# Segment sums of a graph layer: runs of ten edges added up on VectorE, four products of sums per group on TensorE in place of 20

## What is computed

```python
h = relu(layernorm(x))
m_in = concat([h[src], h[dst], edge_attr])            # 160 per edge
msg  = silu(m_in @ W1 + b1) @ W2 + b2                 # 64 per edge
a    = softmax(silu(m_in @ Wa1 + ba1) @ Wa2 + ba2)    # one weight per edge, over ALL edges
agg  = segment_sum(msg * a, dst)                      # per node
out  = x + silu(concat([h, agg]) @ Wu1 + bu1) @ Wu2 + bu2
```

## Time and profile before

| | |
|---|---|
| runs, median of 3 | 2097.85 us (2091.92 to 2098.32) |
| the profiled execution, whole | 2096.55 us |
| its span | 2094.9 us |
| busy share of the span | PE 45%, DVE 52%, ACT 45%, POOL 73% |
| granted TensorE clock, mean | 0.688 of full |
| DMA | 228.43 MB, mean 109 GB/s |

### The profile page before, as it was taken

One profiled execution on the slowest core, in us unless ns is written; L12 is line 12 of the kernel. 1 busy time (PEld: TensorE's weight loads), 2 busy tenths in 40 slices (PEclk: granted clock), 3 DMA queues, 4 the chain that ended last, 5 costly groups with the idle time before them and its releaser, 6 DMA issues.

```text
span 2094.9 us, 21031 instructions
## 1 busy us (share of the span) xinstructions
PE 939.0 (45%) x6771; PEld 878.7 (42%) x6771; DVE 1098.9 (52%) x2367; ACT 933.7 (45%) x1107; POOL 1530.1 (73%) x1628
## 2 busy tenths in 40 slices
PE   6444444444434444444444444444434444444446
PEld 4344444433334444444434444444334344444334
DVE  5555555554554555555455545555545554554556
ACT  3544444454444444444444444444444444444443
POOL 2777777777777777777777777777777777777772
PEclk9667666666666676666666666667666666667668
DMA  7644444444444444444444444444443444444422
GB/s 199 155 122 107 105 110 107 105 105 105 105 111 114 109 105 111 107 105 105 105 105 107 115 112 105 107 109 105 105 105 105 105 116 112 107 105 112 105 69 51
DMA packets 101990, 228.43 MB, mean 109 GB/s; under 512 B 45184, under 2 KB 65460, under 8 KB 91636
## 3 DMA queue, kind: packets, MB, share of 16 engines
q1 hardware_dynamic: 47588, 120.63, 22.2%
q0 software_dynamic: 51584, 105.75, 19.9%
q10 hardware_dynamic: 2704, 0.66, 0.1%
HBM read 218.91 MB, written 8.00 MB: 108 GB/s over the span
## 4 chain that ended last, share of the span: by engine, by line
POOL 72%; issue 24%; PE 2%; DVE 1%; DMA 1%; ACTq 0%; ACT 0%; POOLq 0%; DVEq 0%
POOL p_rows L404 72%; PE bank L584 1%; DMA p_rows<-p_tab,src_all 0%; PE bank L577 0%; PE bank L728 0%; PE bank L738 0%; ACTq L438 0%; DMA q_tab<-s 0%; DMA out<-s 0%; DVE stat L773 0%; DVE bank L917 0%; DVE prod L900 0%; PE bank L677 0%; DVE lgb L926 0%; DVE lg L902 0%
## 5 line engine op out<-in xcount | busy, mean ns | idle before, releaser
L404 POOL DMA_INDIRECT p_rows<-p_tab,src_all x1612 | 1523.1, 945 | 529.3 <-issue 490.1
L636 PE MATMUL bank<-hot,v 128*65 128x96 f32 x3200 | 450.8, 329 | 850.9 <-DVE v L907 850.9
L636 PEld LDWEIGHTS bank<-hot,v 128*65 128x65 f32 x3200 | 435.9, 203 | 870.7 <-DVE v L907 870.7
L917 DVE TENSOR_TENSOR bank<-bank,p_rows 128x512 f32<-128x512 f32 (+1 forms) x403 | 269.4, 669 | 871.5 <-DMA p_rows<-p_tab,src_all 863.7
L524 ACT ACTIVATE s<-bank 128x512 f32<-128x512 f32 x403 | 240.4, 597 | 1021.1 <-DVE bank L917 1020.2
L622 PE MATMUL bank<-q_win,comb 128*128 128x128 f32 x3224 | 442.6, 295 | 266.1 <-ACT s L524 259.5
L622 PEld LDWEIGHTS bank<-q_win,comb 128*128 128x128 f32 x3224 | 407.9, 206 | 287.4 <-ACT s L524 264.7
L492 ACT ACTIVATE comb<-dst_b,row_of 96x1024 f32<-96x1024 int32 (+1 forms) x162 | 217.4, 1342 | 24.8 <-DMA dst_b<-dst_row 24.8
L498 ACT ACTIVATE comb<-comb,ones 96x1024 f32<-96x1024 f32 (+1 forms) x162 | 218.7, 1350 | 2.7
L870 DVE TENSOR_TENSOR hot<-bank,rel 128x960 f32<-128x960 f32 x162 | 178.2, 1139 | 0.0
L900 DVE TENSOR_TENSOR prod<-s,bank 128x512 f32<-128x512 f32 (+1 forms) x162 | 131.6, 813 | 18.6 <-ACT s L524 16.1
(11 more groups left out here) (110 smaller groups left out, 299.1 us busy)
## 6 DMA issues: line engine op xcount, KB each, us to landing
dst_b<-dst_row SPq DMA_DIRECT2D x80, 960.0 KB
p_rows<-p_tab,src_all POOLq DMA_INDIRECT x1612, 2.5
comb<-efT SPq DMA_DIRECT2D x80, 320.0 KB, 3.6
q_win<-q_tab SPq DMA_DIRECT2D x81, 48.0 KB, 2.9
p_tab<-s SPq DMA_DIRECT2D x12, 256.0 KB, 2.3
q_tab<-s SPq DMA_DIRECT2D x12, 256.0 KB, 5.6
out<-s SPq DMA_DIRECT2D x6, 256.0 KB, 2.3
x_sb<-x SPq DMA_DIRECT2D x2, 512.0 KB, 5.2
```

What stands on the lines that cost most here:

```text
L404: pool.indirect_dma_start(p_rows[:, a, t * H2:(t + 1) * H2], None, p_tab, bass.IndirectOffsetOnAxis(src_all[:, g * TG + t:g * TG + t + 1], ...
L636: last = nc.tensor.matmul(ps_part[0:U1, 0:WIN], v[:, t, :], hot[:, t * WIN:(t + 1) * WIN], start=(t == 0), stop=(t == T - 1))
L917: nc.vector.tensor_tensor(ps_z[q][:, n:], ps_z[q][:, n:], p_rows[:, a, q * 512 + n:(q + 1) * 512], ALU.add).then_inc(z_ok, 1)
```

## The change

In the tiles of a group the edges are laid out anew: partition p now holds 20 consecutive edges of the sorted list (edge p*20 + t in tile t), in place of edge t*128 + p. A group is cut into two runs of ten tiles (`RUNS` = 2), so each partition holds two runs of ten consecutive edges. As `dst` is sorted, a run that touches at most two nodes is made of edges equal to its first and edges equal to its last. For groups 0 to 78 DVE makes two sets of weights in PSUM (`w_run`: those of the first node of the run, and the rest), multiplies `s2` with each (two products of 128 x 1300, written with the ten edges of a run side by side, so with a step of ten elements), and reduces each over the ten edges to `run_sum`, four sets of 65 columns. The one-hot matrix is made for the first and last edge of each run only (four in place of 20), and PE makes four products per group in place of 20. Groups 79 and 80 keep one product per tile. `worst_fit` gets a further test, that each run has only edges equal to its first or its last: two comparisons of 128 x 1600, two of 128 x 12, a maximum and a minimum over 128 x 1612 and two short ones. If a run does not fit, the flag sends the kernel down the general path. The left-out parts of the diff rename the semaphores' counts, declare the new tensors, adapt the mask of the doubled edges in the last group to the new layout, and adapt the tail to the new counts.

```diff
@@ -124,7 +126,9 @@
         rel_g = sb("rel_g", [P, 2, TG])
         q_win = sb("q_win", [P, 2, H2])
         p_rows = sb("p_rows", [P, 2, TG * H2])
+        first_run = sb("first_run", [P, C // P])
         hot = sb("hot", [P, TG * WIN])
+        run_sum = sb("run_sum", [P, SEGS, U1])
         comb = sb("comb", [P, 2, TG * P])
         s2 = sb("s2", [P, 2, TG, 2 * U1])
         prod = sb("prod", [P, 3 * TQ, U])
...
@@ -137,13 +141,15 @@
         gmax = sb("gmax", [1, 1])
         neg_max = sb("neg_max", [P, NG])
         fade = sb("fade", [P, 2])
-        v = sb("v", [P, TG, U1])
+        vs = sb("vs", [P, 2, TG * U1])
 
         acc = sb("acc", [U1, NP])
         ref = sb("ref", [U1, NP])
         zall = sb("zall", [P, 1])
         rz = sb("rz", [P, 1])
 
+        v = vs[:, 0].rearrange("p (t u) -> p t u", u=U1)
+        fits = flat(vs)[:, 0:C // P]
         s2_all = s2[:].rearrange("p a t u -> p (a t u)")
         dst_i = s2_all[:, 0:C // P].bitcast(I32)
         rows = s2_all[:, C // P:C // P + RING * NBT * H2].rearrange("p (a t u) -> p a t u", a=RING, t=NBT)
...
@@ -160,6 +166,7 @@
         ps_small = bank[5]
         ps_part = bank[6]
         ps_w = ps_small[:, 2 * P:2 * P + TG]
+        w_run = ps_small[:, 3 * P:3 * P + 2 * TG].rearrange("p (k t) -> p k t", k=2)
         iota_c = bank[7][:, 0:P]
         wa2c = bank[7][:, P:P + U]
         bu2c = bank[7][:, 2 * P:2 * P + D]
...
@@ -255,6 +262,22 @@
 
         def tiles(g):
             return TL if is_last(g) else TG
+
+        def by_tile(g):
+
+            return g >= LAST - 1
+
+        def products(g):
+
+            return tiles(g) if by_tile(g) else SEGS
+
+        def hots_ready(g):
+
+            return g + 1 + max(0, g + 2 - LAST)
+
+        def runs(t, g):
+
+            return t[:, g * TG:g * TG + tiles(g)].rearrange("p (r t) -> p r t", r=RUNS)
 
         def per(a, g, n):
 
...
@@ -625,15 +648,19 @@
 
             def sums(g):
 
-                pe.wait_ge(v_ok, g + 1)
-                pe.wait_ge(hot_ok, 2 * g + 2)
+                pe.wait_ge(hot_ok, hots_ready(g))
                 wait(pe, acc_ok, g)
-                T = tiles(g)
+                if by_tile(g):
+                    pe.wait_ge(v_ok, LAST + g)
+                else:
+                    pe.wait_ge(run_ok, 2 * g + 2)
                 if g == 1:
                     pe.wait_ge(bad_ok, 1)
                     nc.tensor.transpose(ps_part[0:1, P:2 * P], bad[:, 2:3], ident[:])
-                for t in range(T):
-                    last = nc.tensor.matmul(ps_part[0:U1, 0:WIN], v[:, t, :], hot[:, t * WIN:(t + 1) * WIN], start=(t == 0), stop=(t == T - 1))
+                n = products(g)
+                for i in range(n):
+                    what = v[:, i, :] if by_tile(g) else run_sum[:, i, :]
+                    last = nc.tensor.matmul(ps_part[0:U1, 0:WIN], what, hot[:, i * WIN:(i + 1) * WIN], start=(i == 0), stop=(i == n - 1))
                 last.then_inc(part_done, 1)
 
             def group(g, a):
...
@@ -855,7 +882,17 @@
                 chain(nc.vector.tensor_reduce(bad[:, 0:1], rel[:], AX.X, ALU.max))
                 chain(nc.vector.tensor_reduce(bad[:, 1:2], rel[:], AX.X, ALU.min))
                 chain(nc.vector.tensor_scalar(bad[:, 0:1], bad[:, 0:1], float(1 - WIN), None, ALU.add))
-                nc.vector.scalar_tensor_tensor(bad[:, 2:3], bad[:, 1:2], -1.0, bad[:, 0:1], ALU.mult, ALU.max).then_inc(bad_ok, 1)
+                chain(nc.vector.scalar_tensor_tensor(bad[:, 2:3], bad[:, 1:2], -1.0, bad[:, 0:1], ALU.mult, ALU.max))
+                for lo, hi, n in ((0, LAST * TG, TG // RUNS), (LAST * TG, C // P, TL // RUNS)):
+                    of_run = rel[:, lo:hi].rearrange("p (r t) -> p r t", t=n)
+                    for keep, end in ((first_run, 0), (fits, n - 1)):
+                        nc.vector.tensor_tensor(keep[:, lo:hi].rearrange("p (r t) -> p r t", t=n), of_run,
+                                                of_run[:, :, end:end + 1].broadcast_to([P, (hi - lo) // n, n]), ALU.is_equal).then_inc(run_fit, 1)
+                dve.wait_ge(run_fit, 4)
+                chain(nc.vector.tensor_tensor(fits[:], fits[:], first_run[:], ALU.max))
+                chain(nc.vector.tensor_reduce(bad[:, 0:1], fits[:], AX.X, ALU.min))
+                chain(nc.vector.tensor_scalar(bad[:, 0:1], bad[:, 0:1], -1.0, 1.0, ALU.mult, ALU.add))
+                nc.vector.tensor_tensor(bad[:, 2:3], bad[:, 2:3], bad[:, 0:1], ALU.max).then_inc(bad_ok, 1)
 
             def set_flag():
 
...
@@ -863,13 +900,20 @@
                 chain(nc.vector.tensor_tensor(bad1[:, 2:3], bad1[:, 1:2], bad1[:, 0:1], ALU.max))
                 nc.vector.tensor_scalar(flag[:], bad1[:, 2:3], 0.0, None, ALU.is_gt).then_inc(flag_ok, 1)
 
-            def one_hots(g, k):
+            def tile_hots(g, k):
 
                 T = tiles(g)
                 t0, n = k * (T // 2), T // 2
                 nc.vector.tensor_tensor(hot[:, t0 * WIN:(t0 + n) * WIN].rearrange("p (t n) -> p t n", t=n),
                                         iota_c[:, 0:WIN].unsqueeze(1).broadcast_to([P, n, WIN]),
-                                        rel[:, bass.ds(g * TG + t0, n)].unsqueeze(2).broadcast_to([P, n, WIN]), ALU.is_equal).then_inc(hot_ok, 1)
+                                        rel[:, g * TG + t0:g * TG + t0 + n].unsqueeze(2).broadcast_to([P, n, WIN]), ALU.is_equal).then_inc(hot_ok, 1)
+
+            def run_hots(g):
+
+                n = tiles(g) // RUNS
+                nc.vector.tensor_tensor(hot[:, 0:SEGS * WIN].rearrange("p (r k n) -> p r k n", r=RUNS, k=2),
+                                        iota_c[:, 0:WIN].unsqueeze(1).unsqueeze(1).broadcast_to([P, RUNS, 2, WIN]),
+                                        runs(rel, g)[:, :, 0::n - 1].unsqueeze(3).broadcast_to([P, RUNS, 2, WIN]), ALU.is_equal).then_inc(hot_ok, 1)
 
             def set_ref(g, node):
 
...
@@ -906,6 +950,22 @@
                 nc.vector.tensor_reduce(wsum[:, a:a + 1], ps_w[:, 0:T], AX.X, ALU.add)
                 return nc.vector.tensor_tensor(v[:, 0:T, :], s2[:, ab, 0:T, 0:U1], ps_w[:, 0:T].unsqueeze(2).broadcast_to([P, T, U1]), ALU.mult)
 
+            def segment_sums(g, a):
+
+                T = tiles(g)
+                n = T // RUNS
+                here = slice(g * TG, g * TG + T)
+                weighed = [vs[:, k, 0:T * U1].rearrange("p (r u t) -> p r u t", r=RUNS, u=U1) for k in range(2)]
+                nc.vector.tensor_tensor(w_run[:, 0, 0:T], ps_w[:, 0:T], first_run[:, here], ALU.mult).then_inc(w_run_ok, 1)
+                nc.vector.scalar_tensor_tensor(w_run[:, 1, 0:T], first_run[:, here], 0.5, ps_w[:, 0:T], ALU.is_lt, ALU.mult).then_inc(w_run_ok, 1)
+                for k in range(2):
+                    dve.wait_ge(w_run_ok, 2 * g + 1 + k)
+                    nc.vector.tensor_tensor(weighed[k].rearrange("p r u t -> p r t u"), s2[:, a, 0:T, 0:U1].rearrange("p (r t) u -> p r t u", r=RUNS),
+                                            w_run[:, k, 0:T].rearrange("p (r t) -> p r t", r=RUNS).unsqueeze(3).broadcast_to([P, RUNS, n, U1]), ALU.mult).then_inc(v_ok, 1)
+                for k in range(2):
+                    dve.wait_ge(v_ok, 2 * g + 1 + k)
+                    nc.vector.tensor_reduce(run_sum[:, k::2, :], weighed[k], AX.X, ALU.add).then_inc(run_ok, 1)
+
             def add_rows(g, a, q):
 
                 dve.wait_ge(z_done, g * NQ + q + 1)
...
@@ -953,7 +1013,11 @@
 
                 T = tiles(g)
                 dve.wait_ge(w_ok, 2 * g + 2)
-                weigh(T, a, a).then_inc(v_ok, 1)
+                if by_tile(g):
+                    weigh(T, a, a).then_inc(v_ok, 1)
+                else:
+                    nc.vector.tensor_reduce(wsum[:, a:a + 1], ps_w[:, 0:T], AX.X, ALU.add)
+                    segment_sums(g, a)
 
             def group(g, a):
                 late = g > 0
...
@@ -975,8 +1039,7 @@
                 if g > 1:
                     add_part(g - 2, a)
                 if late:
-                    one_hots(g - 1, 0)
-                    one_hots(g - 1, 1)
+                    run_hots(g - 1)
                     weighted(g - 1, 1 - a)
                 if g == LAST - 1:
                     add_rows(g, a, 3)
...
@@ -1145,7 +1208,8 @@
     GE = EDGE_TILES * P
     full = N_EDGES // GE * GE
     last = -(-(N_EDGES - full) // (4 * P)) * 4 * P
-    edges = np.concatenate([np.arange(full), np.arange(N_EDGES - last, N_EDGES)])
+    edges = np.concatenate([np.arange(full).reshape(-1, P, EDGE_TILES).transpose(0, 2, 1).reshape(-1),
+                            np.arange(N_EDGES - last, N_EDGES).reshape(P, -1).T.reshape(-1)])
     src, dst, ef = (np.ascontiguousarray(inputs[n])[edges] for n in ("src", "dst", "edge_attr_32"))
     laid = {
         "src": src.reshape(-1, P).T,
```

More of the change, by code:

```diff
@@ L56, in build @@
     RING = 6
+    RUNS = 2
+    SEGS = 2 * RUNS
     ACT_ODD = 6
     assert NT == NB * NBT + 1 and NT == UB * UT + 1 and NG % 2 == 1 and NB == 12
```

(14 more changed lines are left out.)

10 lines of the change are left out of this document (5 added, 5 removed).

## The result

The changed kernel took 2111.47 us, the median of 15 runs (2095.91 to 2112.67). The kernel before took 2094.34 us in its runs on the same chip (2091.01 to 2107.29). The ratio is 1.0055, with a 95% interval from 1.0041 to 1.0070: slower by 0.55%, about 11.5 us. The ratio weighs all runs. The two medians alone lie 17.1 us apart, because the runs of both kernels fall in clusters (before: eight at 2091 to 2094, five near 2098, two at 2107), and a median jumps from one cluster to the next. The forecast was +4.2 us, inside the 0.3% that can't be told from none; the median lies 2.5 us above the top of the range.

A forecast was written before the change was run, and what follows sets the result against it. The prediction took POOL's chain of gathers as the bound, with all else hidden. Three held gathers add 4.2 us to the profiled 2096.55, giving 2100.75; 1.3 more for the median makes 2102.0 us (+0.2%), range 2095 to 2109.

The forecast's parts named there:

- what bounds the kernel: POOL's 1612 gathers, 0.944 + 0.305 us per step, never waiting for another engine; PE's saved work is worth nothing.
- the test of the fit: Once, between groups 0 and 1: about 8 us on DVE, hidden as delay, but holding gathers by 4.2 us in sum.
- three holds of 1.4 us: Two comparisons and the maximum, each with two SBUF inputs, delay a gather; 4.2 us in sum, ends 1.7 and 5.5.
- the row of 1.58: Before the change, a gather beside line 836, with two SBUF inputs, took 1.58 us more than the median.
- the products: Two DVE products of 128 x 1300 per group, written with a step of ten: 1.49 us each, high end 2.98.
- The group's new work: DVE's added work per group, 0 to 78: 7.2 us, net +3.4, hidden behind the gathers at 16.6 of 25 us.
- The idle stretch in group 79: DVE still idle before group 80's first rows, with 1.9 us to spare, so the new work there costs nothing.
- The first rival: DVE late at group 79 through slower products, lengthening the tail; typical time 2105.5 us, chance 0.24.
- PE's busy time: Over the whole kernel, down to about 590 us, as 16 of 20 products go in groups 0 to 78.
- From there to the end groups 79 and 80 run the old code: After group 80's first rows land, nothing on the way to the end changes, so no cost was added there.
- the tail still 35.7 us: From the start of the last gather to the end, the time stays at 35.7 us, as before the change.
- The clock rival: PE's clock stays at 1.2 GHz in the tail, adding up to 14.8 us: 2117 us; chance 0.02.

The follow-up runs named there:

- e1: The kernel before with only four of the 20 products of sums in groups 0 to 78; ratio 1.0007.
- e2: The kernel before with the further test of the fit alone, its result not used; ratio 1.0019.
- e8: The changed kernel with 64 one-column memsets on DVE in group 40, which move its later code; ratio 1.0003, median 2098.80 us.
- e3: The changed kernel without the test of the fit, each run's first edge copied to PSUM so the comparison has one SBUF input; ratio 1.0065.
- e9: The kernel before with the window bases of the subtraction that makes rel read from PSUM in place of SBUF; ratio 0.9989.
- e10: The kernel before with 64 one-column memsets on DVE in group 40; ratio 1.0046, median 2107.05 us.
- e11: The kernel before with 128 one-column memsets on DVE in group 40; ratio 1.0000.
- e5: The kernel before with two reduces of 1000 columns added on DVE in the tail, right after its branch; ratio 1.0046, median 2108.16 us.
- e6: The changed kernel with four filler products on PE in place of two while DVE is at its branch; ratio 1.0013, median 2101.27 us.
- e4: The changed kernel with the two products written dense and the reduces reading with a step of 65; ratio 1.0060.
- e7: The changed kernel without the general path on all four engines, so that none branches over it; ratio 1.0017.
- e12: The kernel before with the window bases in PSUM and four filler products on PE in place of two; ratio 0.9991.

## Why the prediction was right or wrong

**Right: what bounds the kernel.** The chain is still the gathers, at a median of 945 ns with 0.30 between. PE's saving was worth nothing (e1), and DVE's added work was hidden, as forecast.

**Right in kind, wrong in size: the test of the fit.** The prediction took three holds of 1.4 us, 4.2 in sum, ends 1.7 and 5.5. Measured: 1.96 us in the profile after, 2.64 in e2, 1.78 in e8. The mis-sized term is the 1.4 for each. A held gather ends 0.81 us after its DVE operation, so an operation of 1.82 us adds at most 1.82 + 0.81 - 0.94 = 1.69 us, when the gather begins with it, and the row of 1.58 that the estimate leaned on was near that end. And the three holds are not independent: the first one sets when the next gather begins, so the second and third came out the same in every kernel with the whole test (1.42 to 1.43 and 1.72 to 1.74 us, 1.3 us together over the median), and only the first varied, from 1.44 to 2.32 us. That two SBUF inputs are the cause is shown from both sides: the hold goes when one operand moves to PSUM (e3, e9), at the same 1.81 us on DVE. By the Trainium skill's rule in SBUF — State Buffer, Who interferes with whom, it is an exclusive lock, and the trace agrees in so far as each held gather ended a constant 0.81 us after the operation that held it.

**Wrong in size, without effect: the products.** The prediction took 1.49 us each, with a memset as the nearest row, and carried 2.98 as the high end. Measured: 2.455. The memset of 40 elements was too small a witness. The group's new work is 0.55 + 0.34 + 2 x 2.455 + 2 x 1.475 = 8.75 us and not 7.2, DVE is at 17.3 of 25 us and not 16.6, and its busy time 1456 us, not 1370. The idle stretch in group 79 is 1.44 us and not 1.9. That it came so near has luck in it: the products were 1.9 us longer together, but operations that follow each other on DVE overlap by some 0.1 us in the trace, where the sum had added 0.2 for waits, so the whole stretch (2044.43 to 2053.93) took 9.5 us and not the 10.5 that its single durations add up to. The first rival needed a product of 3.5 us, so it didn't come true even so. The rule of the Trainium skill (Vector Engine (DVE) Microarchitecture Reference, Measured stream behaviour on trn2) would have given 2.3 to 3.4 us, and the trace agrees with it: 2455 ns over 1300 columns are 1.9 ns each.

**A smaller miss: PE's busy time.** Forecast 590 us, measured 682. The saving was counted at the old durations, but the granted clock fell (0.64 against 0.70 in the same stretch), and the remaining products got longer: those of `zmm` take 332 ns in place of 295, 70 us in all. It costs nothing in the middle.

**The step that failed: "From there to the end groups 79 and 80 run the old code", and so "the tail still 35.7 us".** The code is the old one, but it lies at another place, and the prediction priced no branch. The clock rival had the right effect and the right place, "If it stayed at 1.2 GHz in the tail", and nearly the right price (up to 14.8 us; the tail of e3 is 47.0 us instead of 35.7, of which 9.5 come after that gap). It was put at 0.02 because "The work of 2061 to 2075 is not changed". That is true of what is computed, though its first products ran slower (6.21 us in place of 4.88). What decided was a gap just behind them. The chain, link by link:

1. DVE's branch over the general path takes 2.9 us and not 0.6, by the place of the code: e8 takes it away from the changed kernel, e10 gives it to the old one, e11 takes it away again.
2. `acc` is late by 2.3 us, and PE idles 2.4 us, not 1.05, before the first product that needs it. (PE's start slips by 1.4 us only: before, it began 0.9 us later after `acc` than it does here, by a wait that no view explains.)
3. The granted clock then falls to 0.50, and, to judge by the times of the runs, stays there nearly to the end in most executions: e5 makes this with a delay of another kind, e6 prevents it with two more filler products and the branch as slow as ever.

Over e8's ratio of 1.0003 the changed kernel's 1.0055 leaves 0.5% for this chain, some 11 us; the profiles have the tail at 36.1 us in e8 and at 47.0 and 47.9 in e3 and e4. The part that belongs to the change as such, the holds, is 2 us, 0.1%, and would have been "same", as forecast. So the forecast was close for the work that it priced, and missed because the code moved. In the profiled execution after, the clock came back after 3.4 us, hence only 4.1 us: about 0.4 up to the branch, where the sums were slower, 1.4 more until PE's first product behind it, 1.6 in PE's products from there on, with the short stretch at half clock, and 0.7 at the last stores.

**What stays open.** What is fetched behind the branch was not isolated. In all kernels that were slow there, an instruction queue begins a load of 8192 bytes about 1.03 us after the branch and another 3.5 to 3.9 us after it; in the others one load begins 1.2 to 1.4 us after it, when DVE has already gone on. That fits a load of code that has to be waited for, but the first of the slow ones is over 1.4 to 1.6 us after the branch and the second begins only when DVE is at work again, so neither is shown to be what ended the wait of 2.9 us. The Trainium skill (Advanced Engine Details and Errata, Control Flow Timing) gives a compare-and-branch about 108 ns. The trace records 72 ns for the instruction itself, in fast and in slow kernels alike; the 0.60 and 2.86 us, counted to the next instruction, are both much longer, so what differs comes behind it. Open too is why the clock came back in the profile after and not in e3, and why it was lost after 1.27 us of idle time in e7. And the kernel before has runs at 2105 to 2107 as well, two of 15 here; the same loss of the clock would fit them, but none of them was profiled.

## What to carry to other kernels

Before a change of under 1% is credited or blamed, move the code by some do-nothing instructions in both kernels: here 64 memsets of one column were worth 0.5%, a loss in the one kernel and a gain in the other. Where PE waits in a short tail for an engine that has just branched, give it filler work that covers the wait, for a gap of 2.4 us cost some 9 us through the clock. And a one-time VectorE operation beside GpSimd's gathers held them when it read two operands from SBUF, by 0.5 to 1.7 us each; with one of them in PSUM it didn't.

## What the runs showed of the hardware that was not expected

- A compare-and-branch on DVE over a long block took 0.60 to 0.62 us or 2.86 to 3.04 us until the next instruction, by the place of the code: the count of instructions before it, divided by 128, left a remainder of 103 to 111 or of 39 to 43.
- A step costs 0.96 us per 1300 columns in f32 on the output of a product (ten words, 2455 ns) and as much on the input of a reduce (65 words, 2431 ns), against 1504 and 1475 ns without it.
- Profiled executions differ in two things that the edits don't explain. The first gather starts at 41.7 to 42.1 us in e3, e5 and e10 and at 45.5 to 46.0 in the others (40.6 in e12). The mean gather is 943.8 to 946.1 ns in e1 to e11, over 1612 gathers 3.7 us, and goes with the chip: on each of three chips the kernels agree within 0.5 ns. So the start of one event says little about a change of 0.1% unless both profiles come from one chip.
